# Reordering two weight splits in the 128-row tiles of stage one, and halving the contraction of unread products in layer two

## The chip, the cores and the metric

The kernel runs on one core of one Trainium2 chip, as a single launch. The metric is the device time in microseconds from start to end of the program. Its engines here are TensorE (PE, with its weight loads PEld), VectorE (DVE), ScalarE (ACT), GpSimd (POOL) and the DMA queue that SyncE issues (SP). Each engine works through its own list of instructions in order and waits on semaphores.

## The reference

Two layers, each a cross attention and a mixture of experts, on x of shape 2 x 1024 x 256 with a context of 2 x 77 x 256, all in float32:

```
x = x + L0_xattn(layernorm(x), ctx, ctx, w_q, w_kv, w_concat)      # 16 heads of 16
x = x + L0_ffn(layernorm(x), router_w, gate_w, up_w, down_w)       # 8 experts, top 2, hidden 1024
x = x + L1_xattn(layernorm(x), ctx, ctx, Wq, bq, Wk, bk, Wv, bv)   # one head of 256
x = x + L1_ffn(layernorm(x), gate_w, w1, w2, w3, w1s, w2s, w3s)    # 8 experts, top 2, hidden 256, one shared

# L0_ffn, for each expert e:
h  = silu(xf @ gw.T) * (xf @ uw.T)
eo = h @ dw.T
out = out + mask[:, None] * eo * mean_w
```

The experts' inner work is the gated product h of 1024 columns and the down product.

## The kernel before, in words

All float32 products are made in three passes: each operand is split into a high part (rounded to fp32r, made by ScalarE as a copy, line 786) and a low part (the rest, made by VectorE as a subtraction, line 1174), and TensorE adds high x high, high x low and low x high (mm3 and mm3x, lines 337 to 352; all products come from line 335).

The program has, in order: attention of layer 0, the routing, the experts of layer 0 (called stage one here), attention of layer 1, its routing, the experts of layer 1, and the last sums.

**Stage one.** The tokens are sorted by expert into 24 tiles, whose sizes stand in SPAN: (2, 2, 1, 2, 2, 1, 2, 1) three times, 2 for a tile of 256 rows (pair0) and 1 for one of 128 rows (single0). So tiles 2, 5, 7, 10, 13, 15, 18, 21 and 23 have 128 rows. The hidden 1024 columns are worked in four quarters (q = 0 to 3, G0 = 4). A tile's weights are six blocks of 128 x 1024: 0 to 3 are gate and up of the quarters, 4 and 5 the down weights. Each block is loaded by SP into wr (load0, waiting until the low split of the block of the tile before is done), split by ScalarE (w0_hi) and then by VectorE (w0_lo). There is one set of six split blocks, so splits of the next tile run during the present one.

A 128-row tile runs so. On TensorE (line 2251): quarters 0, 1 and 2 (six products of 512 columns each), turn_h of the first half (four transposes of the gated products of quarters 0 and 1), quarter 3, the transposes of the next tile's input, the first half of the down product (down_single, 12 products of 256 columns), turn_h of the second half. The second half of the down product stands behind the first quarter of the next tile. On ScalarE (line 973): the activation of each quarter, and between them w0_hi of the tile's own blocks 4 and 5, the high copy of the turned first half (turned_h_hi), block 0 of the next tile, the high copy of the next input (x_hi0), the turned second half, block 1 of the next tile. On VectorE (line 1592) the same order with the gated product hf (line 1596), w0_lo, turned_h_lo and x_lo0. The order is written out by hand. The order of the splits is also listed in turns_w (line 456), by whose place each wait on w_lo counts; blocks 4 and 5 stand there one behind the other.

The waits around it: turn_h(t, 0) waits for the gated product of quarter 1, down_single(t, 0) for the low part of the turned first half and for the low split of block 4, the first quarter of the next tile for the low part of its input (xe_lo).

**Layer two's start.** After stage one SP loads the expert outputs back (load_y), VectorE adds them to x (add_rows, line 1626), TensorE transposes the sums (turn_summed, line 2281), ScalarE and VectorE split them, and TensorE makes the scores (scores1, products of 78 columns). While TensorE has to wait, it runs products whose results nobody reads: idle_products1, 30 of them before the first turn_summed, 9 before the first scores and 6 before the first turn_weights (lines 2358 to 2363). They read xe_hi, 128 rows, 512 columns, and write bank 5 of the PSUM. TensorE shares one PSUM of eight banks of 512 columns; bank 6 is first used in this stage by the logits.

Of the kernel before, what the change touches and what calls it, by code (L numbers as in the profile page):

```python
# [5 lines left out]
P = 128  # L6
# [72 lines left out]
def build_program(nc, A):  # L79
# [4 lines left out]
    with ctx:  # L84
# [9 lines left out]
        def sb(name, shape, dt=f32, stack=ctx):  # L94
            return stack.enter_context(nc.sbuf_tensor(name, shape, dt))
# [138 lines left out]
        xe_hi, xe_lo = sb("xe_hi", [P, 2, KC, FT], f32r), sb("xe_lo", [P, 2, KC, FT], f32r)  # L234
# [48 lines left out]
        ps = ctx.enter_context(nc.psum_tensor("ps", [P, 8, 512], f32))  # L283
# [49 lines left out]
        def mm(out, w, x, start, stop):  # L333

            return nc.tensor.matmul(out, w, x, start=start, stop=stop, skip_group_check=True)  # L335
# [129 lines left out]
        def parted(t, b):  # L465

            return turns_w.index((t, b)) + 1
# [314 lines left out]
        def _(act):  # L782
            s = nc.scalar

            def copy(o, i):
                return s.activation(o, i, ACT.Copy)  # L786
# [137 lines left out]
            def w0_hi(t, b):  # L924
                act.wait_ge(w_in[b], 16 * (t + 1))
                copy(w_hi[:, b, :], wr[:, b, :]).then_inc(f0["w_hi"], 1)

            def x_hi0(t):
                n = SPAN[t] * P
                act.wait_ge(f0["xt_mm"], t + 1)  # L930
                copy(xe_hi[:, t % 2, :, 0:n], ps[:, 6 + t % 2, 0:KC * n].rearrange("p (c n) -> p c n", c=KC)
                     ).then_inc(f0["xt_hi"], 1)
# [40 lines left out]
            def single0(t):  # L973
                on = t + 1 < T0
                for q in range(G0):
                    act.wait_ge(f0["gu_mm"], G0 * t + q + 1)
                    s.activation(sg[:, q // 2, (q % 2) * FT:(q % 2 + 1) * FT], ps[:, (0, 2, 1, 3)[q], 0:FT], ACT.Silu
                                 ).then_inc(f0["silu"], 1)
                    if q < 2:
                        w0_hi(t, 4 + q)  # L980
                    if q == 2:
                        turned_h_hi(t, 0)
                        if on:
                            w0_hi(t + 1, 0)
                if on:
                    x_hi0(t + 1)
                turned_h_hi(t, 1)
                if on:
                    w0_hi(t + 1, 1)

            def turned_h_hi(t, k):
                act.wait_ge(ht_mm, 2 * SPAN[:t].count(1) + k + 1)
                copy(h_hi[:, k, :, :].rearrange("p c n -> p (c n)"), ps[:, (5, 6 + t % 2)[k], :]).then_inc(f0["h_hi"], 1)
# [5 lines left out]
            for t in range(T0):  # L999
                (single0, pair0)[SPAN[t] - 1](t)  # L1000
# [163 lines left out]
        def _(dve):  # L1164
# [8 lines left out]
            def sub(o, a, b):  # L1173
                return v.tensor_tensor(o, a, b, ALU.subtract)  # L1174
# [374 lines left out]
            def w0_lo(t, b):  # L1549
                dve.wait_ge(f0["w_hi"], parted(t, b))  # L1550
                sub(w_lo[:, b, :], wr[:, b, :], w_hi[:, b, :]).then_inc(f0["w_lo"], 1)

            def x_lo0(t):
                n = SPAN[t] * P
                dve.wait_ge(f0["xt_hi"], t + 1)
                sub(xe_lo[:, t % 2, :, 0:n], ps[:, 6 + t % 2, 0:KC * n].rearrange("p (c n) -> p c n", c=KC),
                    xe_hi[:, t % 2, :, 0:n]).then_inc(f0["xt_lo"], 1)

            def turned_h_lo(t, k):
                dve.wait_ge(f0["h_hi"], parts_of(t, k))  # L1560
                sub(h_lo[:, k, :, :].rearrange("p c n -> p (c n)"), ps[:, (5, 6 + t % 2)[k], :],
                    h_hi[:, k, :, :].rearrange("p c n -> p (c n)")).then_inc(f0["h_lo"], 1)
# [29 lines left out]
            def single0(t):  # L1592
                on = t + 1 < T0
                for q in range(G0):
                    dve.wait_ge(f0["silu"], G0 * t + q + 1)
                    v.tensor_tensor(hf[:, q // 2, (q % 2) * FT:(q % 2 + 1) * FT], ps[:, (0, 2, 1, 3)[q], FT:2 * FT],
                                    sg[:, q // 2, (q % 2) * FT:(q % 2 + 1) * FT], ALU.mult).then_inc(f0["h_mul"], 1)
                    if q < 2:
                        w0_lo(t, 4 + q)
                    if q == 2:  # L1600
                        turned_h_lo(t, 0)
                        if on:
                            w0_lo(t + 1, 0)
                if on:
                    x_lo0(t + 1)
                turned_h_lo(t, 1)
                if on:
                    w0_lo(t + 1, 1)
# [6 lines left out]
            for t in range(T0):  # L1615
                (single0, pair0)[SPAN[t] - 1](t)
# [237 lines left out]
        def _(pe):  # L1854
# [118 lines left out]

            def idle_products1(k):
                for _ in range(k):
                    mm(ps[:, 5, :], xe_hi[:, 0, 0, 0:P], xe_hi[:, 0, :, :].rearrange("p c n -> p (c n)"), True, True)

            def idle_products2(k, b):
                for _ in range(k):
# [376 lines left out]

            pe.wait_ge(f0["y_ok"], halves(T0 - 1, 0))
            idle_products1(30)
            turn_summed(0)
            idle_products1(9)  # L2360
            scores1(0)
            turn_summed(1)
            idle_products1(6)
            turn_weights(0)
            scores1(1)
# [168 lines left out]
```

## Time and profile before

| | |
|---|---|
| median of 3 runs | 816.46 us (815.66 to 816.51) |
| span of the profiled execution | 815.6 us |
| PE busy | 742.3 us, 91% |
| PEld busy | 658.9 us, 81% |
| DVE busy | 593.4 us, 73% |
| ACT busy | 482.5 us, 59% |
| POOL busy | 291.5 us, 36% |
| mean granted TensorE clock | 0.956 |

The profile is of one execution. No time is listed for that execution beside its span, from the first to the last instruction; the median of the runs is 0.9 us above it. Busy is the time in which an engine had an instruction in work. Matmuls overlap in a row of them: the start of one to the start of the next tells the pace, not the duration. The granted clock is told as a share of 2.4 GHz: 1.00 is 2.4 GHz, 0.50 is 1.2 GHz.

### The profile page before, as it was taken

To read this page: it belongs to the slowest core of one execution; us is meant where nothing else is said; L and a number is where in the kernel's file an instruction comes from. 1 tells how busy PE (TensorE), PEld (TensorE's weight loads), DVE (VectorE), ACT (ScalarE), POOL (GpSimd) and SP (SyncE) were. 2 spreads that over 40 slices of the span, in tenths; PEclk is the share of its full clock that TensorE was granted. 3 is DMA by queue.
4 is the path that set the end of the run, shared out by engine and by line. 5 is a ranking of instruction groups with operands and counts; after the bars stand their busy time and mean duration, and the time that the engine had idled before them with its cause. 6 is when DMAs were issued, how large, how long until landed. Compare 5 with 4: busy or idle time off the path is not lost.

```text
span 815.6 us, 13971 instructions
## 1 busy us (share of the span) xinstructions
PE 742.3 (91%) x4973; PEld 658.9 (81%) x4973; DVE 593.4 (73%) x1047; ACT 482.5 (59%) x819; POOL 291.5 (36%) x293
## 2 busy tenths in 40 slices
PE   5898999985999999999999999998888898998984
PEld 5566776764999998999998999997676688887874
DVE  6766765765867868868868868867577767776747
ACT  2566666411567767767767767666236655776751
POOL 9456558302023213122222132220061036777540
PEclk9999999996899999999999999999968989999998
DMA  5000001114766858776857866854600367788738
GB/s 177 1 2 0 28 25 53 53 52 139 280 205 202 280 174 274 226 256 217 277 170 266 249 236 215 283 180 130 213 1 0 108 208 234 247 243 257 244 115 294
DMA packets 56373, 139.01 MB, mean 170 GB/s; under 512 B 6897, under 2 KB 25458, under 8 KB 56306
## 3 DMA queue, kind: packets, MB, share of 16 engines
q1 hardware_dynamic: 48818, 117.67, 43.8%
q0 software_dynamic: 7488, 20.46, 7.8%
q8 instruction: 41, 0.67, 0.3%
q14 instruction: 26, 0.21, 0.1%
HBM read 117.39 MB, written 20.71 MB: 169 GB/s over the span
## 4 chain that ended last, share of the span: by engine, by line
PE 57%; DVE 17%; DMA 8%; ACT 6%; issue 5%; POOL 4%; SPq 1%; POOLq 0%; DVEq 0%; ACTq 0%
PE ps L335 52%; DVE w_lo L1174 7%; DMA wr<-in_w1gu 5%; ACT w_hi L786 3%; POOL p_lo L691 2%; PE ps L2218 1%; DVE h_lo L1174 1%; PE ps L2174 1%; DVE x_a L1191 1%; DMA xnb<-y_d 1%; DMA wr<-y_d 1%; DVE x_all L1626 1%; DVE x_all L1836 1%; PE ps L1946 1%; SPq L568 1%
## 5 line engine op out<-in xcount | busy, mean ns | idle before, releaser
L1174 DVE TENSOR_TENSOR w_lo<-wr,w_hi 128x1024 fp32r<-128x1024 f32 (+2 forms) x193 | 221.7, 1160 | 58.2 <-ACT w_hi L786 57.4
L786 ACT ACTIVATE w_hi<-wr 128x1024 fp32r<-128x1024 f32 (+2 forms) x193 | 192.3, 1000 | 39.6 <-DMA wr<-in_w 22.8
L335 PE MATMUL ps<-xe_hi,w_hi 128*128 128x256 f32 x600 | 174.2, 290 | 4.6 <-DVE xe_lo L1174 3.4
L335 PE MATMUL ps<-xe_hi,w_lo 128*128 128x256 f32 x600 | 171.6, 286 | 0.0
L335 PE MATMUL ps<-xe_lo,w_hi 128*128 128x256 f32 x600 | 171.5, 286 | 0.0
L710 POOL DMA_INDIRECT y_d<-ye,sca x39 | 44.6, 1143 | 278.6 <-ACT ye L941 274.1
L335 PE MATMUL ps<-w_hi,h_hi 128*128 128x256 f32 x422 | 124.3, 295 | 8.3 <-DVE h_lo L1174 6.8
L335 PEld LDWEIGHTS ps<-xe_hi,w_hi 128*128 128x128 f32 x600 | 117.0, 195 | 8.1 <-DVE xe_lo L1174 6.1
L335 PE MATMUL ps<-w_lo,h_hi 128*128 128x256 f32 x422 | 119.2, 282 | 0.0
L335 PE MATMUL ps<-w_hi,h_lo 128*128 128x256 f32 x422 | 119.2, 282 | 0.0
L335 PEld LDWEIGHTS ps<-xe_lo,w_hi 128*128 128x128 f32 x600 | 117.1, 195 | 0.0
L335 PEld LDWEIGHTS ps<-xe_hi,w_lo 128*128 128x128 f32 x600 | 116.9, 195 | 0.0
L335 PEld LDWEIGHTS ps<-w_hi,h_hi 128*128 128x128 f32 x422 | 80.5, 191 | 12.8 <-DVE h_lo L1174 6.7
L335 PEld LDWEIGHTS ps<-w_lo,h_hi 128*128 128x128 f32 x422 | 80.7, 191 | 0.0
L335 PEld LDWEIGHTS ps<-w_hi,h_lo 128*128 128x128 f32 x422 | 80.6, 191 | 0.0
L691 POOL TENSOR_TENSOR p_lo<-p,p_hi 128x512 fp32r<-128x512 f32 (+2 forms) x44 | 56.7, 1291 | 48.2 <-ACT p_hi L904 48.0
L948 ACT ACTIVATE sg<-ps 128x512 f32<-128x512 f32 x60 | 35.7, 595 | 43.7 <-PE ps L335 43.7
L786 ACT ACTIVATE h_hi<-hf 128x512 fp32r<-128x512 f32 x75 | 47.1, 628 | 23.9 <-DVE hf L1568 14.8
L1174 DVE TENSOR_TENSOR h_lo<-hf,h_hi 128x512 fp32r<-128x512 f32 x75 | 51.5, 687 | 8.2 <-ACT h_hi L786 7.4
L702 POOL DMA_INDIRECT xr<-xn_d,gat x39 | 42.6, 1092 | 40.2 <-DVE sca L1518 25.4
L760 POOL DMA_INDIRECT xnb<-xm_d,gat x39 | 41.8, 1072 | 39.1 <-DVE sca L1518 27.6
L1568 DVE TENSOR_TENSOR hf<-ps,sg 128x512 f32<-128x512 f32 x60 | 41.3, 689 | 12.3 <-ACT sg L948 10.1
(342 smaller groups left out, 1528.1 us busy)
## 6 DMA issues: line engine op xcount, KB each, us to landing
wr<-in_w SPq DMA_DIRECT2D x144, 512.0 KB, 4.4
wr<-in_w1gu SPq DMA_DIRECT2D x24, 512.0 KB, 5.0
wr<-in_w1d SPq DMA_DIRECT2D x24, 256.0 KB, 3.2
xn_d<-xnb SPq DMA_DIRECT2D x8, 512.0 KB, 3.5
wr<-y_d SPq DMA_DIRECT2D x8, 512.0 KB, 7.8
x_all<-in_x SPq DMA_DIRECT2D x4, 512.0 KB, 6.3
xm_d<-xnb SPq DMA_DIRECT2D x4, 512.0 KB, 3.0
xnb<-y_d SPq DMA_DIRECT2D x4, 512.0 KB, 5.5
```

The lines of the kernel that those rows point to most:

```text
L335: return nc.tensor.matmul(out, w, x, start=start, stop=stop, skip_group_check=True)
L568: sp.dma_start(wr[:, 2 * (t % 2) + b, 0:n], A[name][ds(e * P, P), :]).then_inc(w_in[2 * (t % 2) + b], 16)
L691: g.tensor_tensor(p_lo[0:w, b % 4, :], p32[0:w, b % 3, :], p_hi[0:w, b % 4, :], ALU.subtract).then_inc(p_ls, 1)
L702: pool.indirect_dma_start(xr[:, t % 2, half, :], None, src, bass.IndirectOffsetOnAxis(ap=gat[n][:, col + half:col + half + 1], axis=0)).th ...
L710: pool.indirect_dma_start(dst, bass.IndirectOffsetOnAxis(ap=sca[n][:, col + half:col + half + 1], axis=0), ye[:, t % 2, half, :], None).th ...
L760: pool.indirect_dma_start(x_ring(t, half), None, xm_d, bass.IndirectOffsetOnAxis(ap=gat[1][:, COL[t] + half:COL[t] + half + 1], axis=0)).t ...
L786: return s.activation(o, i, ACT.Copy)
L948: s.activation(sg[:, q % 2, :], ps[:, q % 2, :], ACT.Silu).then_inc(f0["silu"], 1)
L1174: return v.tensor_tensor(o, a, b, ALU.subtract)
L1191: ins = v.tensor_scalar(n["x"][:, j, :], src(j), n["mv"][:, j, 0:1], n["rs"][:, j:j + 1], ALU.subtract, ALU.mult)
L1568: v.tensor_tensor(hf[:, q % 2, :], ps[:, 2 + q % 2, :], sg[:, q % 2, :], ALU.mult).then_inc(f0["h_mul"], 1)
L1626: ins = v.tensor_tensor(x2g, x2g, landed_last(g, c), ALU.add)
```

## The change

In the 128-row tiles, ScalarE and VectorE no longer work on down-weight block 4 behind quarter 0 and on block 5 behind quarter 1; both splits stand behind quarter 1. The order of the blocks among themselves, and so turns_w and all counts of the semaphores, stays. Nothing changes on TensorE in stage one. In idle_products1 each product over 128 rows becomes two, over rows 0 to 63 into bank 5 and over rows 64 to 127 into bank 6, each of 512 columns.

```diff
--- before.py
+++ after.py
@@ -976,8 +976,9 @@
                     act.wait_ge(f0["gu_mm"], G0 * t + q + 1)
                     s.activation(sg[:, q // 2, (q % 2) * FT:(q % 2 + 1) * FT], ps[:, (0, 2, 1, 3)[q], 0:FT], ACT.Silu
                                  ).then_inc(f0["silu"], 1)
-                    if q < 2:
-                        w0_hi(t, 4 + q)
+                    if q == 1:
+                        w0_hi(t, 4)
+                        w0_hi(t, 5)
                     if q == 2:
                         turned_h_hi(t, 0)
                         if on:
@@ -1595,8 +1596,9 @@
                     dve.wait_ge(f0["silu"], G0 * t + q + 1)
                     v.tensor_tensor(hf[:, q // 2, (q % 2) * FT:(q % 2 + 1) * FT], ps[:, (0, 2, 1, 3)[q], FT:2 * FT],
                                     sg[:, q // 2, (q % 2) * FT:(q % 2 + 1) * FT], ALU.mult).then_inc(f0["h_mul"], 1)
-                    if q < 2:
-                        w0_lo(t, 4 + q)
+                    if q == 1:
+                        w0_lo(t, 4)
+                        w0_lo(t, 5)
                     if q == 2:
                         turned_h_lo(t, 0)
                         if on:
@@ -1973,7 +1975,9 @@
 
             def idle_products1(k):
                 for _ in range(k):
-                    mm(ps[:, 5, :], xe_hi[:, 0, 0, 0:P], xe_hi[:, 0, :, :].rearrange("p c n -> p (c n)"), True, True)
+                    for h in range(2):
+                        at = slice(h * P // 2, (h + 1) * P // 2)
+                        mm(ps[:, 5 + h, :], xe_hi[at, 0, 0, 0:P], xe_hi[at, 0, :, :].rearrange("p c n -> p (c n)"), True, True)
 
             def idle_products2(k, b):
                 for _ in range(k):
```

## Rows read from the trace of the kernel before

**Rows 1.** Windows: length, busy PE, PEld, DVE, ACT, POOL (count), clock, DMA share, GB/s.
```profile
205.50:560.00 354.50, 351.23 (x2678) 335.04 (x2679) 276.24 (x336) 246.89 (x365) 79.18 (x70) 0.99 0.69 232
...
597.40:617.90 20.50, 19.32 (x86) 17.93 (x86) 16.07 (x56) 8.15 (x26) 8.40 (x6) 0.50 0.00 1
577.00:580.20 3.20, 3.20 (x9) 2.53 (x8) 0.00 (x0) 0.00 (x0) 0.00 (x0) 0.50 0.73 239
```

**Rows 2.** Waits in 205 to 573 us: who for whom, us in total, times, longest.
```profile
PE ps L2218 <- DVE hf L1596: 2.7, 9, 0.3
...
ACT w_hi L786 <- DMA wr<-in_w: 1.0, 2, 0.7
```

**Rows 3.** Timeline of tile 2, ScalarE: start, us, engine, line, instruction, idle before.
```profile
245.09 0.38 ACT L977 ACTIVATE sg<-ps 128x256 f32<-128x256 f32 x1 [0.91 <-PE ps L335]
...
246.45 0.38 ACT L977 ACTIVATE sg<-ps 128x256 f32<-128x256 f32 x1
...
246.73 1.05 ACT L786 ACTIVATE w_hi<-wr 128x1024 fp32r<-128x1024 f32 x1
...
247.81 0.39 ACT L977 ACTIVATE sg<-ps 128x256 f32<-128x256 f32 x1
...
248.77 0.60 ACT L786 ACTIVATE h_hi<-ps 128x512 fp32r<-128x512 f32 x1 [0.57 <-PE ps L2218]
...
249.26 1.05 ACT L786 ACTIVATE w_hi<-wr 128x1024 fp32r<-128x1024 f32 x1
...
250.21 0.38 ACT L977 ACTIVATE sg<-ps 128x256 f32<-128x256 f32 x1
```

**Rows 4.** Timeline of tile 2, VectorE.
```profile
245.51 0.42 DVE L1596 TENSOR_TENSOR hf<-ps,sg 128x256 f32<-128x256 f32 x1 [3.24 <-ACT sg L977]
...
246.46 1.23 DVE L1174 TENSOR_TENSOR w_lo<-wr,w_hi 128x1024 fp32r<-128x1024 f32 x1 [0.52 <-ACT w_hi L786]
...
247.60 0.42 DVE L1596 TENSOR_TENSOR hf<-ps,sg 128x256 f32<-128x256 f32 x1
...
247.94 1.22 DVE L1174 TENSOR_TENSOR w_lo<-wr,w_hi 128x1024 fp32r<-128x1024 f32 x1
...
249.07 0.42 DVE L1596 TENSOR_TENSOR hf<-ps,sg 128x256 f32<-128x256 f32 x1
...
249.40 0.69 DVE L1174 TENSOR_TENSOR h_lo<-ps,h_hi 128x512 fp32r<-128x512 f32 x1
...
250.35 1.23 DVE L1174 TENSOR_TENSOR w_lo<-wr,w_hi 128x1024 fp32r<-128x1024 f32 x1 [0.26 <-ACT w_hi L786]
...
251.82 0.68 DVE L1174 TENSOR_TENSOR xe_lo<-ps,xe_hi 128x512 fp32r<-128x512 f32 x1
```

**Rows 5.** Timeline of tile 2 and the start of tile 3, TensorE.
```profile
247.39 0.39 PE L335 MATMUL ps<-w_hi,xe_lo 128*128 128x512 f32 x1
...
248.07 0.66 PE L2218 MATMUL ps<-ident,hf 128*128 128x128 f32 x4 [0.30 <-DVE hf L1596]
...
250.31 0.36 PE L335 MATMUL ps<-w_hi,h_hi 128*128 128x256 f32 x1
...
252.56 0.39 PE L335 MATMUL ps<-xe_hi,w_hi 128*128 128x256 f32 x1
```

**Rows 6.** Timeline of tile 23, TensorE, first half of the down product.
```profile
567.26 0.19 PEld L335 LDWEIGHTS ps<-w_hi,h_hi 128*128 128x128 f32 x1 [0.53 <-issue]
```

**Rows 7.** Timeline of layer two's start: weight loads of the unread products, and around them.
```profile
576.35 8.27 PEld L335 LDWEIGHTS ps<-xe_hi 128*128 128x128 f32 x30 [3.99 <-DVE w_lo L1174]
...
581.81 2.49 DVE L1626 TENSOR_TENSOR x_all<-x_all,wr 128x1024 f32<-128x1024 f32 x2 [5.51 <-DMA wr<-y_d]
...
584.66 1.03 PEld L2281 LDWEIGHTS ps<-ident,x_all 128*128 128x128 f32 x8
...
585.65 1.90 PEld L335 LDWEIGHTS ps<-xe_hi 128*128 128x128 f32 x9
...
595.13 0.43 PEld L2296 LDWEIGHTS ps<-ident,p 128*77 128x77 f32 x4 [2.67 <-ACT p L1022]
```

## The prediction

> **What bounds the kernel now.** I read the stretches first, then the waits, then one 128-row tile instruction by instruction. In stage one (205.5 to 560 us) TensorE is busy for 351.2 of 354.5 us at granted clock 0.99 [rows 1]: here a microsecond taken from TensorE is one of the kernel, and a microsecond by which it is held is one too. The list of waits shows what little holds it: nine waits of 0.3 us on the gated product of VectorE, one per 128-row tile; the loads almost never hold anything (ScalarE waited for one twice, 1.0 us together) [rows 2]. So nothing downstream, no transfer above all, would swallow a delay made inside stage one.
>
> The second edit lies behind stage one, where TensorE has little to do and 45 unread products fill its time. There the granted clock matters: it is 0.50 (1.2 GHz) while the first of them run, and again 0.50 from 597.4 to 617.9 us with TensorE busy 19.3 of 20.5 us [rows 1].
>
> **Edit one, ScalarE.** The reader should follow tile 2. ScalarE reads quarter 0 at 245.09, splits block 4, and reads quarter 1 at 246.45 [rows 3]. An activation takes 0.28 us to the next instruction (246.45 to 246.73), a split 0.95 (249.26 to 250.21); so with block 4 in between it was free at 245.09 + 0.28 + 0.95 = 246.32, and waited for TensorE until 246.45: quarter 1's activation cannot come sooner. After it the new order is two splits in a row: 246.73 and 246.73 + 0.95 = 247.68; quarter 2's activation then starts at 248.63 where it was 247.81. The turned half is copied 0.28 later, at 248.91, before 248.77; the next tile's block 0 follows 0.49 later, at 249.40, before 249.26. On ScalarE the move costs only 0.14 us.
>
> **Edit one, VectorE.** It runs in order, and here it is the tighter engine. Pitches from [rows 4]: activation to product 0.42 (245.09 to 245.51), product to next 0.34, low split to next 1.14 (246.46 to 247.60), low split after its high split 1.09 (249.26 to 250.35), h_lo to next 0.60 (its 0.69 less the 0.09 by which each of the others follows sooner than its duration). Before, it starts block 4 at 246.46, and from there to the end of xe_lo at 252.50 it has one gap, 0.26 us. After:
> - product of quarter 1: 246.45 + 0.42 = 246.87 (was 247.60);
> - low split of block 4: its high split starts 246.73, + 1.09 = 247.82 (was 246.46). VectorE stands empty between, about 0.6 us, and before the product for another 0.9 us;
> - low split of block 5: 247.82 + 1.14 = 248.96 (was 247.94);
> - product of quarter 2: 250.10 (was 249.07);
> - h_lo of the first turned half: 250.43 (was 249.40), so + 1.03, ending 251.12;
> - low split of the next tile's block 0: its high split would allow 249.40 + 1.09 = 250.49, but VectorE comes at 250.43 + 0.60 = 251.03 (was 250.35). The gap before it (shown as 0.26; 0.35 start to start) takes up 0.35 of the 1.03; the rest stays: + 0.68;
> - xe_lo of the next tile: 251.82 + 0.68 = 252.50, ending 253.18.
> No work is added. Two splits, 2.28 us, are put behind an instruction that waits for TensorE, and the engine has no room later to catch up.
>
> **Edit one, TensorE.** The gain is real: the last product of quarter 2 starts at 247.39, pitch 0.23, so the four transposes of the first half could start at 247.62 instead of 248.07 [rows 5], 0.45 us sooner, a little more than the wait of 0.30. It is lost at the next wait. Quarter 3 and the transposes of the next input end 0.45 sooner, at about 249.86; the first half of the down product (250.31 before) now needs h_lo, ready at 251.12, and starts at about 251.17. From - 0.45 it has gone to + 0.86. The twelve products, the second turn (held by the product of quarter 3) and then the first quarter of the next tile, which started at 252.56 right behind xe_lo (ending 252.50) [rows 4, 5], come out at 253.24: + 0.68 us. The following 256-row tile is dense TensorE work, whose waits on ScalarE and VectorE all move along with it; I give nothing back there. Queues: SP's loads into blocks 4 and 5 wait for those low splits and go out 1.36 and 1.02 us later, 0.7 and 0.3 after the shift of everything else; loads have slack [rows 2], price nothing. POOL's gathers and scatters hang on TensorE's transposes and ScalarE's outputs and only shift.
>
> Eight tiles of this kind (2, 5, 7, 10, 13, 15, 18, 21): 8 x 0.68 = 5.4 us. Tile 23 is the last: it has no next block 0 and no next input, and TensorE already waited 0.53 us directly on h_lo [rows 6], so it takes the whole 1.03 us. Sum of edit one: + 6.5 us. Bounds: 5.0 if the pitches run 0.2 us better each time, 7.7 if the 0.86 us at the down product were not worked off at all (9 x 0.86).
>
> **Edit two.** 45 products of 512 columns over 128 rows become 90 over 64 rows, two by two on different rows, into banks 5 and 6. Neither bank is in use there. The first 30 end at 584.62 [rows 7], with VectorE's sum (581.81 + 2.49) done at 584.30: any lengthening of this group is on the path almost at once. The 9 have 1.90 us (0.21 each at full clock) against the next low split and fit exactly; the 6 stand before a wait until 595.13 of 2.67 us and cost nothing up to double. The trace has no product pair on separate rows, so: lower bound, a pair takes as long as one does now, 0; upper bound, it takes two, 30 x 0.21 = 6.3 us in the first group and some tenths in the second (the softmax work of VectorE hides most of the other 1.9), near + 6.5. I take the lower end with + 0.2 for entering and leaving the form: the two halves share neither rows nor bank, and per column that goes in, the array's work is that of the row of 0.21 us.
>
> The Trainium skill, "TensorE: Matmul & The Clock Gate", section Part 3: Packing small matmuls, states that products on different row groups run at the same time, started some 4 ns apart. No row here shows it; by that rule edit two is worth zero. "TensorEngine Tiling (Array Packing)", Key Properties, adds that a change of tiling mode drains TensorE, which speaks for a small loss at each of the three groups.
>
> Forecast: 816.46 + 6.5 + 0.2 = 823.1 us. The sum is made in the profiled execution, whose span is 815.6 us; the median of the runs is 0.9 above that, and I carry the difference over.
>
> **Rivals.**
> - Halves one after the other: + 6.5 from edit two, 829.5 us. For it: nothing in the trace shows otherwise. Against: separate rows and banks. Chance 0.15.
> - The halves do not raise the clock. The first group would stay at 1.2 GHz, where it is at granted clock 0.50 now for only 3.2 us [rows 1]: at twice the 0.21 us of [rows 7], 30 take 12.6 us in place of 8.27, + 4.3; the transposes, the 9 and the scores behind them at half clock add about 4 more (1.03 + 1.90 us and some 2.6 of scores, doubled, less 1.5 hidden by VectorE's statistics): 823.1 + 8.3 = 831.4 us. For it: the clock did stay down for 20 us under narrow products. Chance 0.06.
> - The halves hold the clock up where it now falls at 597.4. VectorE is busy 16.07 of these 20.5 us [rows 1], so at most 4.4 us come back, likelier 3: 820.1 us. Chance 0.11.
> - Faster: VectorE has room, and only the wait goes. Then 9 x 0.45 = 4.0 us are won, 812.4 us. For it: the nine waits, and the empty stretch before quarter 0's product. It decides at one point: h_lo of the first half must be done before TensorE asks at 249.86. By the rows it is done 1.26 us later, as four VectorE instructions stand in between. Chance 0.04.
> - The change does nothing (waits of other kinds hide it): 816.5, chance 0.02.
>
> **How the numbers follow.** The forecast case has 0.62. The range 820.0 to 830.0 holds it with its own bounds, the serial halves and half of the case with the clock held, 0.82 in all; out are the clock that stays low and the cases at or below 816.5. A difference under 0.2% (1.6 us) can't be told from none. Faster 0.04, the one case; same 0.03, the change without effect and 0.01 for a held clock that gives back all it can; slower 0.93.
>
> **What would show it.** In the profile after: the nine waits of TensorE's turn on the gated product gone, and nine new ones of 1.2 to 1.4 us on h_lo ahead of the down products; quarter 2's activation on ScalarE directly behind two splits; VectorE idle around 0.5 us between quarter 1's product and block 4; from one group of eight tiles to the next, which holds three 128-row tiles, 3 x 0.68 = 2.0 us more. In layer two: 60 halves that last 8.3 to 8.7 us together, and the turn of the first sums still within 0.4 us of VectorE's sum. I am wrong if the down products do not wait, if the following 256-row tile is shorter than before, or if the 60 halves last 14 us.

## The result and the profile after

The changed kernel ran 818.97 us by the median of 5 (818.69 to 823.85), the kernel before 815.66 (5 runs, 814.52 to 816.51): ratio 1.0051, 95% interval 1.0028 to 1.0073. It is slower, as forecast, but by 3.3 us where 6.6 were forecast, and 818.97 lies below the range of 820.0 to 830.0. Two more measurements of the same kernel, told below, gave 1.0076 (1.0054 to 1.0098) and 1.0118 (1.0077 to 1.0158). The profiled execution of the first measurement was its longest, 823.85 us, with a span of 822.1; the other four took 818.7 to 820.5 us and left no profile.

Tile 2 in the changed kernel; first the timeline of ScalarE, VectorE and the transposes of TensorE (start, duration, engine, line, instruction, idle before).

```profile
243.86 0.38 ACT L977 ACTIVATE sg<-ps 128x256 f32<-128x256 f32 x1 [0.91 <-PE ps L335]
...
245.22 0.38 ACT L977 ACTIVATE sg<-ps 128x256 f32<-128x256 f32 x1 [0.98 <-PE ps L335]
...
245.50 2.00 ACT L786 ACTIVATE w_hi<-wr 128x1024 fp32r<-128x1024 f32 x2
245.63 0.42 DVE L1597 TENSOR_TENSOR hf<-ps,sg 128x256 f32<-128x256 f32 x1 [0.94 <-ACT sg L977]
...
246.38 0.60 PE L2222 MATMUL ps<-ident,hf 128*128 128x128 f32 x4
246.59 2.36 DVE L1175 TENSOR_TENSOR w_lo<-wr,w_hi 128x1024 fp32r<-128x1024 f32 x2 [0.53 <-ACT w_hi L786]
...
247.40 0.37 ACT L977 ACTIVATE sg<-ps 128x256 f32<-128x256 f32 x1
...
247.66 0.60 ACT L786 ACTIVATE h_hi<-ps 128x512 fp32r<-128x512 f32 x1
...
248.86 0.42 DVE L1597 TENSOR_TENSOR hf<-ps,sg 128x256 f32<-128x256 f32 x1
...
249.20 0.68 DVE L1175 TENSOR_TENSOR h_lo<-ps,h_hi 128x512 fp32r<-128x512 f32 x1
...
249.79 1.21 DVE L1175 TENSOR_TENSOR w_lo<-wr,w_hi 128x1024 fp32r<-128x1024 f32 x1
...
251.26 0.68 DVE L1175 TENSOR_TENSOR xe_lo<-ps,xe_hi 128x512 fp32r<-128x512 f32 x1
```

To compare with [rows 3, 4], measure from quarter 0's activation, 243.86 here and 245.09 there. Quarter 1's activation comes 1.36 us behind it in both, now with 0.98 us of idle ahead: the move does not bring it forward. The low split of block 4 comes at 2.73 (was 1.37), h_lo at 5.34 (was 4.31), xe_lo at 7.40 (was 6.73). The whole list of waits of TensorE's products from 205 to 581 us, the line of the same list in the kernel before that has to be compared with it, and two products of TensorE in the changed kernel, the first of the down product and the first of the next tile:

```profile
PE ps L335 <- DVE h_lo L1175: 13.6, 13, 1.7
PE ps L335 <- DVE xe_lo L1175: 4.1, 1, 4.1
```

```profile
PE ps L335 <- DVE h_lo L1174: 2.3, 4, 1.5
```

```profile
250.02 0.36 PE L335 MATMUL ps<-w_hi,h_hi 128*128 128x256 f32 x1 [1.21 <-DVE h_lo L1175]
...
251.99 0.39 PE L335 MATMUL ps<-xe_hi,w_hi 128*128 128x256 f32 x1
```

The nine waits of the turn on the gated product [rows 2] are gone. In their place the down product waits for h_lo: 1.21 us here, in all 13 times for 13.6 us, where the kernel before had 4 times for 2.3 us. Eight of the nine new waits are 1.21 or 1.22 us; in tile 23 it is 1.66. The next tile's first quarter starts 8.13 us behind quarter 0's activation; before it was 7.47 [rows 3, 5]: + 0.66 us.

Layer two's start, from the timeline of TensorE and of its weight loads, first before and then after, and windows (length, busy PE, PEld, DVE, ACT, POOL, granted clock, DMA share, GB/s) that answer to [rows 1]:

```profile
576.36 8.69 PE L335 MATMUL ps<-xe_hi 128*128 128x512 f32 x30 [3.79 <-DVE w_lo L1174]
584.88 1.03 PE L2281 MATMUL ps<-ident,x_all 128*128 128x128 f32 x8
585.68 2.30 PE L335 MATMUL ps<-xe_hi 128*128 128x512 f32 x9
...
590.42 1.09 PE L2281 MATMUL ps<-ident,x_all 128*128 128x128 f32 x8
591.27 1.63 PE L335 MATMUL ps<-xe_hi 128*128 128x512 f32 x6
595.14 0.66 PE L2296 MATMUL ps<-ident,p 128*77 128x128 f32 x4 [2.24 <-ACT p L1022]
```

```profile
581.48 8.70 PE L335 MATMUL ps<-xe_hi 64*128 64x512 f32 x60 [3.79 <-DVE w_lo L1175]
590.11 0.86 PEld L2285 LDWEIGHTS ps<-ident,x_all 128*128 128x128 f32 x8 [0.35 <-issue]
590.11 1.09 PE L2285 MATMUL ps<-ident,x_all 128*128 128x128 f32 x8
591.13 2.34 PE L335 MATMUL ps<-xe_hi 64*128 64x512 f32 x18
...
596.10 1.09 PE L2285 MATMUL ps<-ident,x_all 128*128 128x128 f32 x8
597.12 1.66 PE L335 MATMUL ps<-xe_hi 64*128 64x512 f32 x12
600.36 0.66 PE L2300 MATMUL ps<-ident,p 128*77 128x128 f32 x4 [1.57 <-ACT p L1023]
```

```profile
204.90:563.00 358.10, 347.66 (x2670) 334.20 (x2670) 274.98 (x335) 243.90 (x365) 77.27 (x70) 0.99 0.70 230
602.40:622.90 20.50, 19.64 (x88) 18.30 (x87) 15.49 (x55) 7.59 (x24) 8.61 (x6) 0.51 0.01 1
```

60 halves last 8.70 us, where 30 whole ones lasted 8.69; 18 last 2.34 (before 2.30), 12 last 1.66 (before 1.63). These are durations from the first start to the last end. From start to start, the way from the first unread product to the second turn of the sums took 14.06 us before and 14.62 after: + 0.56. Before, the weight load of the first turn starts 0.22 us ahead of its first product (584.66 in [rows 7], 584.88); behind the halves it starts with it, at 590.11, after 0.35 us in which nothing was loaded. At the turn of the attention weights 0.1 us of this is left (18.78 us behind the first unread product before, 18.88 after): TensorE waits there in both.

TensorE's idle time in stage one has grown from 3.3 to 10.4 us, more than the stage has lengthened; the profile models the ends of products, so the stretches from start to start are the better measure. The long stretch at half clock is there as before, five microseconds later.

### The profile page after: what moved, and what is told of

The parts are those of the page before. It is cut to its first block, busy times and chain, and to the rows that moved or that the text cites. A ratio compares the mean times of both kernels' runs of the same rounds, so it can differ in the third digit from the quotient of the medians.

```text
span 822.1 us, 14061 instructions
## 1 busy us (share of the span) xinstructions
PE 741.6 (90%) x5018; PEld 659.3 (80%) x5018; DVE 593.2 (72%) x1047; ACT 480.5 (58%) x819; POOL 290.4 (35%) x293
## 4 chain that ended last, share of the span: by engine, by line
PE 57%; DVE 19%; DMA 8%; ACT 6%; issue 5%; POOL 4%; SPq 1%; POOLq 0%; DVEq 0%; ACTq 0%
PE ps L335 53%; DVE w_lo L1175 8%; DMA wr<-in_w1gu 5%; ACT w_hi L786 3%; DVE h_lo L1175 2%; POOL p_lo L691 2%; DVE x_a L1192 1%; DVE hf L1798 1%; DMA xnb<-y_d 1%; DMA wr<-y_d 1%; DVE x_all L1628 1%; DVE x_all L1838 1%; PE ps L1948 1%; ACT h_hi L786 1%; POOL rs_b L598 1%
## 5 line engine op out<-in xcount | busy, mean ns | idle before, releaser
L760 POOL DMA_INDIRECT xnb<-xm_d,gat x39 | 43.8, 1124 | 39.7 <-DVE sca L1519 28.1
```

Of the source, the lines that this page charges most:

```text
L760: pool.indirect_dma_start(x_ring(t, half), None, xm_d, bass.IndirectOffsetOnAxis(ap=gat[1][:, COL[t] + half:COL[t] + half + 1], axis=0)).t ...
```

## The experiments

Each has the kernel before as its base. The ratios are against the kernel before on the same chip. Beside them stands what stage one shows without the rest of the program: from quarter 0's activation in tile 2 to that in tile 23, which holds eight 128-row tiles with what follows them.

```
kernel                     ratio (95%)               tile 2 to 23, us   per 128-row tile
before                                               317.06
both edits (first)         1.0051 (1.0028-1.0073)    322.40             +0.67
both edits (second)        1.0076 (1.0054-1.0098)    322.43             +0.67
both edits (third)         1.0118 (1.0077-1.0158)    322.49             +0.68
split order alone          1.0072 (1.0049-1.0095)    322.42             +0.67
halves alone               0.9996 (0.9977-1.0015)    317.03              0.00
VectorE's order alone      1.0000 (0.9980-1.0019)    317.55             +0.06
ScalarE's order alone      1.0135 (1.0105-1.0166)    327.93             +1.36
block 4 first              0.9932 (0.9906-0.9957)    312.92             -0.52
halves, same rows          1.0343 (1.0308-1.0379)    317.06              0.00
gap filled                 0.9972 (0.9952-0.9993)    317.03              0.00
block 4 first, gap filled  0.9914 (0.9880-0.9947)    312.93             -0.52
```

**The two edits apart, and both again.** The first has the diff's two parts in stage one and the old idle_products1, the second the reverse.

> Edit one alone: both down-weight splits behind quarter 1, the unread products as before. Theory A (the split order costs what the pitches say, 8 x 0.68 + 1.03 = 6.5 us, and edit two gives some 3 us back, since the changed kernel is only 3.3 us slower): + 6 to + 7 us against the kernel before, nine waits of 1.2 us on h_lo, 41 % of which is nowhere given back. Theory B (the order costs only about 3 us in most executions, and edit two is worth nothing): + 3 to + 4 us, the same as both edits together.

> Edit two alone: the order of the splits as before, the 45 unread products as 90 halves. Theory A: 3 us faster than before, with the time won in layer two. Theory B: within 1 us of before; a pair takes as long as one whole product (60 halves in 8.7 us in the profile of the changed kernel), so no work changes its length.

> The changed kernel once more, since the profiled execution of it was 5 us longer than its median. Both theories: + 3.3 us by the median. If executions of one kernel differ in where the granted clock falls, the profile of this run has other low stretches than the first one (602 to 623, 626 to 630 and 636 to 640 us), and a span nearer 817.

The split order alone had a median of 822.80 us, the halves alone 815.99, both 822.64, the kernel before 816.06 (17 runs). So theory A is right about the first edit, + 6.7 us, and wrong about the second, which gives nothing back; theory B is right about the second alone. Both edits together are the sum of the two, + 6.6. The + 3.3 us of the first measurement did not come again. The second profile of the changed kernel has a span of 820.7 us and its low stretches in other places than the first one, from 603.9 to 610.8 and from 614.2 to 624.4 us.

**Which engine's order it is.** Each has the new order on one engine alone:

```diff
 # VectorE's order alone: in the vector single0
-                    if q < 2:
-                        w0_lo(t, 4 + q)
+                    if q == 1:
+                        w0_lo(t, 4)
+                        w0_lo(t, 5)
 # ScalarE's order alone: in the scalar single0
-                    if q < 2:
-                        w0_hi(t, 4 + q)
+                    if q == 1:
+                        w0_hi(t, 4)
+                        w0_hi(t, 5)
```

> Only VectorE's order is the new one (gated products of quarters 0 and 1, then both low splits); ScalarE splits block 4 behind quarter 0 as before. If the 6.5 us come from the high split of block 4 that comes 1.36 us later, so that VectorE starts its backlog later (theory A), little of them is left here: block 4's low split can start at 247.21 instead of 246.46, the product ahead of it is done already, and h_lo of the first half comes 0.42 us later than before while TensorE asks 0.45 sooner; at the next tile + 0.07 us. Sum 8 x 0.07 + 0.4 = + 1.0 us. If it is the order on VectorE itself that costs (theory B): + 6.5 us.

> Only ScalarE's order is the new one (both high splits behind quarter 1's activation); VectorE still has block 4's low split ahead of quarter 1's product, and so waits for it with that product behind. Theory A (the late high split is what costs): the turn of the first half waits until the product at 248.96 + 0.42, 1.3 us later than before, and xe_lo of the next tile comes 1.0 us later; 8 x 1.0 + 1.3 = + 9 us, more than both together (+ 6.6). Theory B (VectorE's order is what costs): + 1 us or less.

VectorE's order alone costs 0.06 us per tile, where + 0.07 was expected, and nothing that shows in the time (medians 816.39 and 815.32, ratio 1.0000). TensorE waits 0.6 us per tile for h_lo there, in place of the 0.30 at the turn, and so gives the 0.45 us back. ScalarE's alone costs 1.36 us, where 1.0 was expected, + 11 us by the ratio (+ 13 by the medians). In its tile 2, timeline:

```profile
244.83 0.38 ACT L977 ACTIVATE sg<-ps 128x256 f32<-128x256 f32 x1 [0.98 <-PE ps L335]
...
245.11 2.00 ACT L786 ACTIVATE w_hi<-wr 128x1024 fp32r<-128x1024 f32 x2
...
246.19 1.23 DVE L1175 TENSOR_TENSOR w_lo<-wr,w_hi 128x1024 fp32r<-128x1024 f32 x1 [1.88 <-ACT w_hi L786]
...
247.34 0.42 DVE L1597 TENSOR_TENSOR hf<-ps,sg 128x256 f32<-128x256 f32 x1
...
247.81 0.66 PE L2219 MATMUL ps<-ident,hf 128*128 128x128 f32 x4 [1.66 <-DVE hf L1597]
...
250.08 1.23 DVE L1175 TENSOR_TENSOR w_lo<-wr,w_hi 128x1024 fp32r<-128x1024 f32 x1 [0.25 <-ACT w_hi L786]
```

VectorE stands empty for 1.88 us until block 4's high split is done, and quarter 1's product, ready since 245.25, waits behind it; TensorE's turn then waits 1.66 us. The gap ahead of the next block's low split is still 0.25, as in [rows 4]: that high split hangs on the turn, and is late with it. My estimate had taken this gap as room to catch up, hence 1.0 for 1.36. Theory A holds: the late high split costs, and the new order on VectorE softens it, from 1.36 to 0.67.

**Starting the backlog sooner.**

```diff
 # on both engines: before the loop over q
+                w0_hi(t, 4)          # VectorE: w0_lo(t, 4)
 # inside, ScalarE
-                    if q < 2:
-                        w0_hi(t, 4 + q)
+                    if q == 0:
+                        w0_hi(t, 5)
 # inside, VectorE
-                    if q < 2:
-                        w0_lo(t, 4 + q)
+                    if q == 1:
+                        w0_lo(t, 5)
```

> The kernel before with the split of block 4 of a 128-row tile ahead of quarter 0's activation on both engines, and block 5 behind quarter 0 on ScalarE and behind quarter 1 on VectorE; unread products as before. If VectorE's backlog is what rules the tile (theory A), starting it about 1.2 us sooner, in the 3.2 us in which VectorE stands empty ahead of quarter 0, takes away the wait of 0.30 us at the turn and no wait on h_lo comes for it: 0.4 us per tile, nine tiles, 812 us against 815.7, 3 to 4 us faster. If the order on VectorE does not rule the tile (theory B), no change.

811.19 us against 816.06: 4.9 us faster, ratio 0.9932, where 3 to 4 were expected; 0.52 us per tile in stage one, where 0.4 was expected. The list of waits of TensorE's products in stage one is now this whole one:

```profile
PE ps L335 <- DVE xe_lo L1175: 3.8, 1, 3.8
...
PE ps L335 <- DVE h_lo L1175: 2.2, 4, 1.5
```

The 3.8 us stand ahead of the first tile, and the four waits are those of the 256-row tiles and of the end, which the kernel before had too. What starts the backlog, in its timeline:

```profile
239.62 1.05 ACT L786 ACTIVATE w_hi<-wr 128x1024 fp32r<-128x1024 f32 x1
...
240.63 0.39 ACT L978 ACTIVATE sg<-ps 128x256 f32<-128x256 f32 x1
...
240.70 1.23 DVE L1175 TENSOR_TENSOR w_lo<-wr,w_hi 128x1024 fp32r<-128x1024 f32 x1 [2.90 <-ACT w_hi L786]
```

The high split lies in ScalarE's 0.91 us ahead of quarter 0 [rows 3], the low one in VectorE's 3.24 us [rows 4].

**Where the halves read.**

```diff
-                        at = slice(h * P // 2, (h + 1) * P // 2)
+                        at = slice(0, P // 2)
```

> The kernel before with every unread product of layer two as two halves that both read rows 0 to 63, into banks 5 and 6; the order of the splits as before. If the pairs of edit two cost no more than one product because their rows are disjoint (theory A), these pairs take double: 60 in 14 to 15 us instead of 8.7, the turn of the first sums 6 us later, + 6 us in the median. If a half product costs half whatever its rows (theory B): 60 in 8.7 us and no change.

844.44 us against 815.32, + 29 us, five times what theory A expected. From its timeline, and its windows:

```profile
576.17 25.54 PE L335 MATMUL ps<-xe_hi 64*128 64x512 f32 x60 [3.79 <-DVE w_lo L1174]
601.64 1.97 PE L2283 MATMUL ps<-ident,x_all 128*128 128x128 f32 x8
603.54 8.05 PE L335 MATMUL ps<-xe_hi 64*128 64x512 f32 x18
```

```profile
576.20:601.70 25.50, 25.50 (x61) 19.41 (x61) 4.41 (x11) 0.00 (x0) 1.04 (x1) 0.51 0.51 165
601.70:625.00 23.30, 23.30 (x77) 18.75 (x76) 8.46 (x20) 3.75 (x12) 10.37 (x5) 0.50 0.00 0
625.00:648.00 23.00, 22.16 (x101) 20.98 (x100) 16.00 (x55) 8.00 (x24) 3.03 (x3) 0.50 0.00 1
```

There are two effects. The halves run one after the other, and the clock stays at 1.2 GHz: 25.54 / 60 = 0.43 us each, twice the 0.21 us of a product at full clock [rows 7], in a stretch in which TensorE is busy all the time. Both the serial halves and the clock that is not raised, two of the prediction's rivals, happen here, with shared rows. It is no accident of the profiled execution: all four took 844.0 to 846.5 us, at a mean clock of 0.931 to 0.940. Why the clock stays down is not shown. The Trainium skill, "TensorE: Matmul & The Clock Gate", section Part 3: Packing small matmuls, has products of different row groups run at the same time, and weight loads overlap products only where the row groups differ. By that rule the trace agrees: 60 in 8.70 us on disjoint rows, one after the other on the same.

**The pause ahead of the fall of the clock.**

```diff
-            idle_products1(6)
+            idle_products1(16)
```

> The kernel before with 16 instead of 6 unread whole products ahead of the first turn of the attention weights, so that TensorE is busy in the 2.67 us in which it waits there, and nothing asks for it. If the fall of the granted clock near 597 us comes from that pause (theory A), the clock stays at 1.00 behind it in most executions and some 3 us come back: 813 us. If it comes from the narrow products of the scores that follow (theory B): the low stretch is there as before, median within 1 us of before.

812.75 us against 815.32, ratio 0.9972: 2 to 3 us faster, with an interval that ends at 0.9993. Its windows (length, busy PE, granted clock, DMA share, GB/s):

```profile
584.00:594.00 10.00, 10.00 (x74) 1.00 0.20 63
594.00:600.00 6.00, 4.46 (x27) 0.68 0.01 1
600.00:614.00 14.00, 13.47 (x65) 0.53 0.01 1
614.00:620.00 6.00, 5.72 (x44) 1.00 0.00 1
```

```profile
597.21 1.14 PE L2296 MATMUL ps<-ident,p 128*77 128x128 f32 x4 [1.54 <-ACT p L1022]
```

TensorE has no pause from 584 to 594, and the clock falls all the same: at 596.2 us, 24.1 us behind the first unread product, where it was 21.0 before. But another pause has opened, the 1.54 us ahead of the second turn of the weights, and the fall lies in it. So filling the first pause does not keep the clock up, but a kernel without a pause was not made, and whether a pause makes the fall is not settled. The clock is down for 17.1 us where it was 20.5 before; the split order alone, whose pause is not filled, had 17.1 us too. Theory A is refuted in that the clock did not stay up, theory B is wrong on the time. Where the 2 to 3 us come from, if they are more than scatter, is not settled.

**The best two together, and a third look at both edits.**

> Block 4 ahead of quarter 0 (e4, 5 us faster) and 16 unread products ahead of the first turn of the weights (f3, 2.3 us faster). The two lie in different stages: if both gains are real they add, 7 us, 808 to 809 us. If the 2.3 us of f3 were only scatter of where the clock falls: 5 us, 811 us.

> The changed kernel a third time. The first time its median was + 3.3 us against the kernel before, the second + 6.6; edit one alone gave + 6.7 and edit two alone nothing. If the second is right (theory A): + 6 to + 7 us. If there is an advantage of the halves that shows only sometimes (theory B): + 3 to + 4 us again.

This chip runs the kernel before in 834.65 us. Stage one is as long here as elsewhere (312.93 and 322.49 us in the table); the two profiles lose their time behind it, 170.4 and 168.1 us from the first expert weights of layer two to the end, where the ten others have 150.6 to 153.8. Why is not settled, and the kernel before was not profiled on this chip. Block 4 first with the gap filled has the lowest ratio, 0.9914 (828.65 us), 6.0 us faster where 7 or 5 were expected; its interval, 0.9880 to 0.9947, holds the product of the two single ratios, 0.9904, but also the 0.9932 of block 4 first alone, so whether the gains add is not shown. The changed kernel was 1.0118 times as long, + 9.8 us, outside of what either theory expected, with a wide interval (1.0077 to 1.0158, + 6.4 to + 13.2 us) whose lower end is the first theory's. No advantage of the halves shows.

## Why the prediction was right or wrong

**Edit one, ScalarE: right.** Quarter 1's activation waits for TensorE and does not move. Quarter 2's came 3.54 us behind quarter 0's, as worked out (248.63 - 245.09).

**Edit one, VectorE: right to 0.02 us at every step shown.** Block 4's low split + 1.36 (forecast 1.36), h_lo + 1.03 (1.03), xe_lo + 0.67 (0.68). That the backlog is the cause was argued; the two single orders and the earlier start show it: what counts is when VectorE can begin the splits.

**Edit one, TensorE: right.** The turn came 0.46 us sooner against quarter 0's activation (forecast 0.45), and the gain was lost at the down product, which started 0.94 us later than before (forecast 0.86) and was held for 1.21 us (forecast: nine waits of 1.2 to 1.4; measured: eight of 1.21 or 1.22 and one of 1.66, in tile 23). Over eight tiles + 5.34 us (forecast 5.4). Tile 23: from its first activation to the first unread product 15.22 us, before 14.21, + 1.01 (forecast 1.03). Sum 6.35 us for a forecast of 6.5. One slip in the bounds: 0.2 us less for each of the nine tiles gives 4.7, not 5.0.

**Edit two: right in the main, and the price of changing the form is real.** By their durations the three groups changed by 0.01, 0.04 and 0.03 us. From start to start TensorE pays more: from the first unread product to the second turn of the sums the changed kernel took 14.62 and 14.66 us in its first two profiles, the kernels with whole products 14.06 to 14.16 in seven. Of this + 0.5 us at most 0.1 reaches the turn of the attention weights; the forecast had + 0.2. In the two other profiles with halves on disjoint rows, halves alone and both edits the third time, the first group took 9.67 and 9.97 us, because the clock had fallen ahead of its first product and 5.5 and 6.2 us of the group ran at half clock, against 3.6 to 4.6 in the nine others; whether halves raise the clock later than whole products, or the fall only came at another place, is not separated. The choice of the lower end was made on disjoint rows and banks; the experiment on shared rows shows that the rows decide. Whether shared banks alone would matter was not tried.

**What was wrong: the step from the profiled sum to the time.** The prediction added its 6.7 us to a fixed level ("816.46 + 6.5 + 0.2", "I carry the difference over") and let its range of 820.0 to 830.0 hold only the costs of the edits; the scatter of executions it put at nothing. The sum itself was right, 6.35 us in the profiles for 6.5. The level was 815.66 us in the five runs beside the changed kernel, 0.8 us lower, and 815.66 + 6.35 makes 822.0 us, where 818.97 was measured: 3.0 us less than the edits cost. Where these 3.0 us went stays open, since only the longest of the five executions was profiled. Nor is the difference carried over a fixed one: in the profiled executions with a listed time this lies 1.7 to 1.8 us above the span, so by that the profile before would be of an execution near 817.3 us, itself 0.9 above the median. Executions of one and the same kernel spread more than that: the kernel before from 812.89 to 818.99 us in 17 runs on one chip, and there the longer ones are those with the lower mean granted clock (correlation - 0.81). The profiles show where:

```
                      start to    tile 2 to   tile 23 to     from there
profile of            tile 2      tile 23     first unread   to the end
before                245.1       317.1       14.2           239.3
both edits (first)    243.9       322.4       15.2           240.6
both edits (second)   244.8       322.4       15.2           238.2
split order alone     245.0       322.4       15.2           238.7
halves alone          241.4       317.0       14.2           238.4
```

The start of the program up to stage one took 201.4 to 205.5 us. The stretch from the first unread product to the first expert weights of layer two took 86.9 us before, 89.0 in the first profile of the changed kernel, 86.7 in the second and 87.4 with the halves alone. It goes with the time at half clock: from 10 to 80 us behind the first unread product the granted clock was 0.50 for 27.3 us in four profiles (the first of the changed kernel, each engine's order alone, block 4 first), and the stretch took 88.7 to 90.3 us; in the seven others (the halves on the same rows left out) it was 0.50 for 17.1 to 20.5 us, and the stretch took 85.8 to 87.9. The changed kernel stands in both lists. Stage one's tiles, in contrast, repeat to 0.03 us over eight of them (317.06 and 317.03, 322.40 and 322.43), and to 0.09 with the third profile, from another chip. The three ratios of the changed kernel, 1.0051, 1.0076 and 1.0118, are estimates of one thing; the split order alone, without the halves, gave 1.0072. Four of the five executions of the first measurement lay at 818.7 to 820.5 us, at clock 0.961 to 0.963; the second had 821.6 to 823.3 at 0.957 to 0.962. The clock speaks for part of that. Why the first five stood so together stays open; an advantage of the halves does not explain it, since alone they gave 0.9996.

**The rivals.** Faster (the backlog has room) is refuted by 1.21 us of wait at the very point named. The clock held by the halves: from 10 to 80 us behind the first unread product the time at half clock was 20.5 us before, 27.3, 17.1 and 20.5 in the three profiles of the changed kernel, 17.1 with the halves alone, and 17.1 with the split order alone, which has no halves; what the halves might do to it does not stand out of that.

## What to carry to other kernels

Before moving work behind an instruction that waits, write down when each engine could begin the work, not only when it must be finished: here the wait of 0.30 us on TensorE was removed by making VectorE, which had 0.26 us of room, begin 1.36 us later. The same rows pointed to the other direction, into the 3.24 us in which VectorE stood empty, and that gave 0.52 us per tile. A forecast of under 1% needs the scatter of the executions in its range (812.89 to 818.99 us for one kernel here). The length of the changed stage itself, which repeats to 0.03 us here, tells what such a change costs; the median of five executions tells it badly.

## What was not expected of the hardware

Products over 64 rows that all read the same 64 rows did not raise the clock: TensorE was busy for all of 25.5 us from 576.2 on and the granted clock stayed at 0.50, and it was still 0.50 at 648 us, whereas with the same number of halves on alternating rows, and with 30 whole products, it was at 1.00 again 3.6 to 6.2 us behind the first of them. The low rate then lasted 72 us, and this, not the doubled products alone, made 29 us. And in a row of them a pair of 64-row products on disjoint rows takes the time of one 128-row product, to within 0.04 us a group where the clock was low equally long (60 in 8.70 us, 30 in 8.69). Going into and out of that form costs some 0.5 us over the first two groups: behind the halves the first weight load of the turn comes after 0.35 us without one, where behind whole products it starts 0.22 us ahead of its product.
